# Second dense node stage of a four-layer GNN: the bias enters PSUM through ScalarE instead of through a bias product on TensorE

## The reference, cut to what matters

```python
h = gatv2_conv(x, s, d, Wl1, Wr1, att1, b1)
h = layer_norm(h, g1, be1)
h = jax.nn.relu(h + x)
h2 = gatv2_conv(h, s, d, Wl2, Wr2, att2, b2)
h2 = layer_norm(h2, g2, be2)
return h2 + h          # and the network adds its own x to it
```

## Time and profile before

| | |
|---|---|
| median of 3 executions | 4792.28 us (4786.27 to 4793.47) |
| profiled execution | 4799.01 us |
| its span (first to last instruction) | 4797.0 us |
| busy over the span | PE 71%, DVE 68%, ACT 56%, POOL 60% |
| mean granted TensorE clock | 0.829 of 2.4 GHz |
| second run of `conv_nodes` | from 1447.84 us (first instruction) to the next stage's first at 1722.86 us |

### The profile page before, as it was taken

One profiled execution on the slowest core, in us unless ns is written; L12 is line 12 of the kernel. 1 busy time (PEld: TensorE's weight loads), 2 busy tenths in 40 slices (PEclk: granted clock), 3 DMA queues, 4 the chain that ended last, 5 costly groups with the idle time before them and its releaser, 6 DMA issues. The chain is left out here.

```text
span 4797.0 us, 66181 instructions
## 1 busy us (share of the span) xinstructions
PE 3393.7 (71%) x14380; PEld 1894.6 (39%) x14380; DVE 3285.1 (68%) x10437; ACT 2668.4 (56%) x7608; POOL 2889.3 (60%) x2835
## 2 busy tenths in 40 slices
PE   1544188544998979997797999948855649974332
PEld 1534133222665633432564344325532215543331
DVE  1322199775996768887786888869978868874332
ACT  1422299796776757775575777726657735530000
POOL 4777687687984457773687555315567600027776
PEclk9656599655999989998898999979978869985555
DMA  8433288796668966664896444459979956753331
GB/s 290 124 97 92 102 282 278 290 406 252 201 190 269 307 194 209 212 212 143 273 323 217 154 158 157 135 195 338 337 239 342 336 164 216 229 185 105 98 99 53
DMA packets 685509, 1019.82 MB, mean 213 GB/s; under 512 B 109779, under 2 KB 293748, under 8 KB 683248
## 3 DMA queue, kind: packets, MB, share of 16 engines
q1 hardware_dynamic: 617296, 877.29, 55.0%
q0 software_dynamic: 65856, 113.13, 9.0%
q10 hardware_dynamic: 2016, 25.69, 1.3%
HBM read 640.44 MB, written 381.14 MB: 213 GB/s over the span
## 5 line engine op out<-in xcount | busy, mean ns | idle before, releaser
L984 DVE TENSOR_TENSOR conv_logits_leaky<-conv_logits_z,conv_logits_sloped 128x512 f32<-128x512 f32 x784 | 516.9, 687 | 117.8 <-ACT conv_logits_sloped L918 102.0
L918 ACT ACTIVATE conv_logits_sloped<-conv_logits_z 128x512 f32<-128x512 f32 x784 | 459.1, 596 | 175.9 <-PE conv_logits_z L880 123.5
L1250 PE MATMUL conv_aggregate_part<-conv_aggregate_weighed,conv_wlc 128*128 128x512 f32 x784 | 360.0, 602 | 39.8 <-DVE conv_aggregate_weighed L1332 39.8
L880 PE MATMUL conv_logits_z<-conv_logits_hdT,conv_logits_wsum 128*128 128x512 f32 x784 | 368.0, 613 | 4.7 <-DVE conv_logits_leaky L984 2.7
L887 PE MATMUL conv_logits_z<-conv_diffT,conv_logits_wl 128*128 128x512 f32 x784 | 352.9, 593 | 0.0
L1570 ACT ACTIVATE conv_nodes_squares<-conv_nodes_o_ps 128x128 f32<-128x128 f32 x784 | 206.5, 278 | 165.7 <-PE conv_nodes_o_ps L1492 165.7
L1332 DVE TENSOR_TENSOR conv_aggregate_weighed<-conv_aggregate_alpha,conv_diffT 128x512 f32<-128x512 f32 x392 | 259.8, 722 | 9.5 <-DMA conv_aggregate_alpha<-ALPHA 9.5
L117 POOL DMA_INDIRECT AGG<-gine_edges_rows,idx x196 | 194.0, 990 | 103.1 <-issue 101.9
L1492 PEld LDWEIGHTS conv_nodes_o_ps<-conv_nodes_wmean,conv_nodes_hT 128*128 128x128 f32 x1568 | 191.3, 192 | 160.3 <-DVE conv_nodes_hT L1528 81.4
L1959 PE MATMUL mean_edges_turned<-mean_edges_ident,mean_edges_hs 128*128 128x128 f32 x196 | 54.6, 434 | 277.7 <-DMA mean_edges_hs<-H,idx 277.7
L111 POOL DMA_INDIRECT gat_logits_hs<-H,idx x196 | 214.4, 1094 | 59.8 <-issue 56.8
(11 more groups left out here) (294 smaller groups left out, 10205.0 us busy)
## 6 DMA issues: line engine op xcount, KB each, us to landing
conv_aggregate_alpha<-ALPHA SPq DMA_DIRECT2D x392, 256.0 KB, 5.3
HX<-gine_finish_hx SPq DMA_DIRECT2D x98, 512.0 KB, 11.7
AGG<-gine_edges_zero ACTq DMA_DIRECT2D x14, 1792.0 KB, 34.2
gine_mlp_x<-x SPq DMA_DIRECT2D x98, 256.0 KB
gine_mlp_agg<-AGG SPq DMA_DIRECT2D x98, 256.0 KB
YT<-gine_mlp_yT SPq DMA_DIRECT2D x98, 256.0 KB, 4.2
gine_finish_x<-x SPq DMA_DIRECT2D x98, 256.0 KB, 7.1
gine_finish_yT<-YT SPq DMA_DIRECT2D x98, 256.0 KB, 11.5
```

The lines of the kernel that those rows point to most:

```text
L880: pe.matmul(z[h][:, :], wsum[:, h * D:(h + 1) * D], hdT[j % 3][:, :], start=True, stop=True).then_inc(z_done[0], 1)
L918: act.activation(sloped[(H * (2 * j + c) + h) % S][:, :], z[h][:, :], ACT.Copy, scale=SLOPE).then_inc(sloped_made[c], 1)
L984: dve.tensor_tensor(leaky[H * c + h][:, :], z[h][:, :], sloped[(H * (2 * j + c) + h) % S][:, :], ALU.max).then_inc(leaky_made[c], 1)
L1250: last = pe.matmul(part[n % 2][:, :], g.wlc[:, h * D:(h + 1) * D], weighed[n % 2][:, h, :], start=(h == 0), stop=(h == H - 1))
```

## The change

In the `final` run only: before the first tile TensorE computes the bias product once into each of the four banks `o_ps` (`start=True, stop=True`). ScalarE copies bank 0 into an SBUF tile `bias_rows` (128x512). From then on ScalarE's step `preload(n)` writes `bias_rows` into the PSUM bank of tile `n`, ahead of `copy_turned(n)` in its step order, and TensorE's `project(n)` waits for that and issues only the four 128x128x128 products, which add to what lies in the bank. `preload(n)` waits until `scale(n - 4)` has read the bank. The first run of `conv_nodes` is built as before.

```diff
+        preloaded, bias_rows = m.sem("preloaded"), m.sb("bias_rows", [P, TILE]) if final else None
...
                     pe.wait_ge(row_made, 1)
+                    for j in range(4):
+                        last = pe.matmul(flat(o_ps[j]), ones[:, :], bias[:, :], start=True, stop=True)
+                    last.then_inc(preloaded, 1)
...
                     past(pe, scaled_made, n - 3)
                     o = o_ps[n % 4]
-                    pe.matmul(flat(o), ones[:, :], bias[:, :], start=True, stop=False, skip_group_check=True)
+                    if final:
+                        pe.wait_ge(preloaded, n + 3)
+                    else:
+                        pe.matmul(flat(o), ones[:, :], bias[:, :], start=True, stop=False, skip_group_check=True)
                     pe.wait_ge(hT_made, n + 1)
...
                 act.wait_ge(set_once, 1)
 
+                if final:
+                    act.wait_ge(preloaded, 1)
+                    act.activation(bias_rows[:, :], flat(o_ps[0]), ACT.Copy).then_inc(preloaded, 1)
+                    act.wait_ge(preloaded, 2)
+
+                def preload(k, i):
+
+                    n = i * NB + k
+                    past(act, scaled_made, n - 3)
+                    act.activation(flat(o_ps[n % 4]), bias_rows[:, :], ACT.Copy).then_inc(preloaded, 1)
...
-                steps = ([(0, copy_turned)] if final else []) + [(1, square), (1, root)] + ([] if final else [(4, relu)])
+                steps = ([(0, preload), (0, copy_turned)] if final else []) + [(1, square), (1, root)] + ([] if final else [(4, relu)])
```

## The result

The changed kernel takes 4776.05 us (median of 11 runs, 4769.96 to 4782.64), the kernel before 4792.91 us (11 runs, 4786.27 to 4811.8). The ratio is 0.9966, 95% interval 0.9957 to 0.9974: 16.9 us less (by the ratio 16.3, from 12.5 to 20.6), against 19 us forecast and 4773 us as the time. It is faster by more than the 0.2% that can be told from no change.

What follows compares the result with a forecast made beforehand. TensorE (PE) bounded the stage at 2.575 us per tile; with the start's 3.1 us and 97 periods of 2.35, squares(97) come 19.0 us earlier: 4792.3 - 19.0 = 4773 us. Range 4767 to 4782, for 8 in 10 4763 to 4794.

Steps and rivals of the forecast that it cites:

- PE is no longer last; ACT is, without a gap: Second dense stage: PE would need 1.525 us per tile, and ACT, at 2.35 us, would run without idle time.
- The period, 2.35 us: ACT's round per tile: squares and root 1.375, copy 0.48, preload 0.50 us; 2.35 used, bounds 2.335 and 2.565.
- The unknown term: ScalarE's preload, an activation from SBUF to PSUM that no earlier row showed: 0.50 us, bounds 0.48 and 0.71.
- The wait of preload for scale(n - 4) and the handshake cost nothing: Scale ends over 2.85 us after its squares, preload comes 8.4 us after them; ACT - PE - ACT has 0.95 us slack.
- Transfers are just below: Three transfers per tile, 786,432 bytes, would take 2.33 us or less, just under ACT's 2.35.
- The start costs 3.1 us (bounds 1.3 to 5.1): Four bias products before the first tile, 6.0 us, would move squares(0) from 1465.65 to 1468.75 us.
- The sum: Squares(97) would start at 1696.7 us against 1715.65, 19.0 us earlier, making the kernel's time 4773 us.
- The rule against the change: With PE busy 65% of each period its clock may be lowered, making PE last again at 2.86 us per tile.
- the slower rival: The clock falls in turn and project: 2.86 us per tile, squares(97) 30.5 us later, 4823 us; chance 0.06.
- Transfers as the pace: 306 GB/s is the limit in the stage: the period stays 2.575 us, 4795 us in all; chance 0.10.
- A dear write to PSUM: The preload's write costs its bound of 0.71 us: period 2.565 us, 4794 us in all; chance 0.07.
- A handshake that costs a tenth: ACT is not gapless, ACT - PE - ACT costs a tenth: period 2.45 us, 9.3 us gained, 4783 us; chance 0.11.

Runs made afterwards that it cites:

- e8_split: The changed kernel with each preload split into two activations of 128x256, the same data: 4782.67 us, ratio to before 0.9977, period 2.457 us.
- e11_limit: e1_no_preload with make_base(n) waiting one finish longer, as in e9_shift: 4753.54 us (one run), period 2.117 us.
- e2_no_x: The changed kernel without the load of x in the second dense stage, the base being h + h: 4779.5 us, ratio to before 0.9967, period 2.362 us.
- e6_k1: The changed kernel with eight more bias products over one row ahead of the four at the stage's start: 4795.86 us (one run).
- e7_k128: The changed kernel with eight products over 128 rows added ahead of the four bias products at the stage's start: 4778.85 us (one run).
- e3_both: The changed kernel with ScalarE's preload kept and TensorE's bias product per tile put back: 4805.22 us, ratio to before 1.0016, period 2.576 us.
- e5_mixed: The changed kernel with one bias product at the start, ScalarE preloading only odd tiles from 5 on, the other tiles using TensorE's product: 4757.69 us, ratio 0.9929.
- e1_no_preload: The changed kernel without preload, so the bias is left out and banks accumulate: 4757.87 us, ratio to before 0.9925, period 2.145 us.
- e9_shift: e5_mixed with make_base(n) waiting for the finish of tile n - 6 instead of n - 7: 4759.65 us, ratio to before 0.9926.

## Why the prediction was right, step by step

- *PE is no longer last; ACT is, without a gap.* Right, by the row of the changed kernel (207.11 of 210.00 us) and by e8_split, which put 0.095 us on ACT and found 0.095 in the period.
- *The period, 2.35 us.* 2.36 measured. The unknown term, an activation from SBUF to PSUM, was put at 0.50 (bounds 0.48 and 0.71) and is 0.52 start to start, 582 ns long. The Trainium skill's estimate from "ScalarE: Activation LUTs", section "What ACT_TABLE_LOAD costs", was 0.52 for each of the two; the preload agrees with it start to start, though it is shorter (582 ns) and overlaps less (0.06 us), and the copy at 0.47 does not. The nearest row by kind (L1583, 0.51) was the better guide than the dearest one.
- *The wait of preload for scale(n - 4) and the handshake cost nothing.* Right: PE waits for ACT 0.8 us per tile and ACT for nobody, and the projections end 0.99 us before their squares start (forecast 0.95).
- *Transfers are just below.* Right in the sign, wrong in the size: they were bounded at 2.25 to 2.33 us, and in e11_limit a tile's three transfers pass every 2.16. The rates that I read at a full share (338 and 350 GB/s) were no ceiling, since 364 pass there; and SyncE's issuing, which the rows point to as the next limit, was not in the forecast at all. It did not matter here, since ACT was above either value. e2_no_x shows that they had no part in the 2.36.
- *The start costs 3.1 us (bounds 1.3 to 5.1).* This term was mis-sized: 5.34 us, above its own upper bound. Of the 2.24 us that it was off, 1.13 are the products, 7.13 us instead of 6.0, and 0.87 the first tile's projections with their signal, 2.07 us (1465.17 to 1467.24) instead of 1.20; the rest is in signals. Both have one cause, the clock. I let the clock rise because TensorE would be busy from 1459.64 on, and the products that keep it busy are over one row, which e6_k1 shows not to count.
- *The sum.* 19.0 forecast, 16.5 measured: 2.2 us for the start, 1.2 us for a period that was 0.012 us too short over 96 tiles, and 0.9 us back, because the last tile's squares have no preload and no copy ahead of them (1694.01 to 1695.42, 1.41 us), which the sum had overlooked. That it offsets part of the two misses is luck.
- *The rule against the change.* The clock stayed at 1.00 through the stage with PE busy 66% of the time, so the slower rival did not come. Whether the transposes helped to hold it, as the stretch in the earlier trace rows says, or the projections alone would have done, no run here separates. (The forecast counted 1.23 us of transposes in that stretch; its two rows overlap, and together they cover 1.06 of the 1.79 us.)
- *The rivals.* Transfers as the pace: refuted by e2_no_x. A dear write to PSUM: refuted by its 582 ns. A handshake that costs a tenth: refuted by ACT's missing idle time and the 0.99 us above.

## What to carry to other kernels

When a term is moved from the full engine to one with room, price the new period as the larger of the two and put the whole engine's round in it, start to start: here 1.05 us came off TensorE, and 0.21 was gained, since ScalarE's own round with the move was 2.36 us. The better move was to divide it: with every other tile's bias on each engine the period fell to 2.155 us, close to the 2.16 at which SyncE issues a tile's transfers. Count the engine that issues transfers among those that can be full: the busy rows don't show it, its waits do. And what is put ahead of the first tile is paid at once: 5.3 us there are as much as 0.055 us in each of 98 tiles. Look there for idle time first.

## What the runs showed of the hardware that I had not expected

- Products over one row kept TensorE busy but did not raise its clock: 20.8 us at 1.2 GHz in e6_k1, against 2.4 GHz after 3.1 us of products over 128 rows in e7_k128 (one execution each). There it fell again after 3.6 us of one-row products and 1.1 us of transposes, with TensorE full. Mixed work can stay low as well: in e3_both TensorE was full for 28 us at 1.2 GHz, and in the first tiles one-row products took 2.0 us of each 4.9. The kernel before, with the same mix, came up 7 us after its first transposes, so what decides is open.
- VectorE's 128x512 addition takes 0.68 us alone and 1025 ns on average when it starts beside GpSimd's addition (e5_mixed; 1027 in e1_no_preload), and one wait, moved by one tile, decides which it is (e9_shift). The Trainium skill, "SBUF — State Buffer", section "Who interferes with whom", says that the two engines share a pair of SBUF ports under an exclusive lock; the runs agree with that. In the 138 such additions of the two runs VectorE's ends 0.55 us after GpSimd's, whether they overlap by 0.31 us or by 1.2, and GpSimd's keeps its 1.27 us; the price is 0.34 us per addition on average.
- A DMA share of 1.00 was read at 306 and at 338 GB/s, 1.02 at 329 and 1.08 at 364: the share says little on how much more will pass. From issue to landing `x` took 4.9 us before, 5.1 in the changed kernel and 6.1 in e11_limit.
- SyncE's issuing of two loads and a store of 256 KB takes it 2.01 us at its shortest (e11_limit), 2.16 on average there and 2.13 in the kernels before and after. The rows point to that as the next limit; no run tests it.
